# Zero fills beside two attentions on ScalarE's queue, first expert's weights loaded in the routing, first rows on ScalarE's queue, biases added after the rows

## The chip, the cores and the metric

The kernel runs on one core of one Trainium2 chip. The metric is the device time of one execution in microseconds (us); lower is better. Of the kernel before there are three timed executions and one profiled one. Engines are named as in the profile: PE is TensorE, PEld its weight load, DVE is VectorE, ACT is ScalarE, POOL is GpSimd, SP is SyncE; a q behind the name means its sequencer, which issues DMAs.

## The reference

Four layers, each a cross attention and a feed-forward part, are added one after the other to `x` (16 batches, 112 rows, 256 wide); the context `ctx` has 16 batches of 375 rows. All is float32. Cut to the parts that the change touches:

```python
# layer 0: focused linear attention (top 11 of 16 per head), then 8 experts, gated
x = x + L0_xattn(layernorm(x), ctx)
xn = layernorm(x) * ln_gamma + ln_beta
top_v, top_i = top_k(xn @ router_w.T, 2);  top_p = softmax(top_v)
slot = e * 560 + pos if pos < 560 else E * 560       # pos: place within expert e, C = 560
buf = zeros(E * C + 1, D).at[slot].set(xn[tokens])   # unused slots stay zero
g, u = split(buf[e] @ w12[e].T);  yb = (silu(g) * u) @ w3[e].T
x = x + scatter_add(yb[slot] * top_p * kept)
# layer 1: tanh-capped attention, shared feed-forward with low-rank terms
# layer 2: softmax attention, 16 heads of 64, K and V from ctx @ w_kv; then
logits = x' @ router_w.T + router_b                  # x' = layernorm(x), top 2 of 8, softmax
out = sum over chosen e of (gelu(x' @ w1[e].T + b1[e]) @ w2[e].T + b2[e]) * cw
x = x + layernorm(out + x') * ln_w + ln_b            # eps 1e-12
# layer 3: softmax attention, 16 heads of 16, with bq, bk, bv, bo; then a ternary feed-forward
x = x + softmax(q k.T / 4) v @ Wo.T + bo
```

## The kernel before

The program is a row of stages, each a block in which every engine runs its own instruction list; a stage ends when all engines have ended it. `x_sb` holds all 16 batches on chip with the 112 rows on the partitions. In order of time, from the span's start: focused attention of layer 0 (0 to 311 us), routing of layer 0 (311 to 426), experts of layer 0 (to some 870), tanh attention, shared experts, wide softmax attention of layer 2 (1255 to 1882), routing of layer 2 (1883 to 2003), experts of layer 2 (2004 to 2271), narrow attention of layer 3 (from 2277), ternary feed-forward (2683 to the end).

**Spilled keys and values.** The wide attention needs K and V of 1024 columns for each batch. For batches 0 to 7 PE projects them early, in holes of the focused attention (batches 0 to 3) and in the routing of layer 0 (batches 4 to 7); `SpilledKeysValues` does it. For each batch there are 8 parts of K and 6 of V: PE projects a part (L2375, L2379), ACT copies it out of the bank (`take`, L2396 and L2399) into a slot `ks` or `vs`, and SP stores the whole batch to DRAM (`serve`: one store `kd` of 1500 KB, L2342, and three stores `vd` of 500 KB, L2347). There are `SLOTS = 3` slots each; before ACT writes the first part of batch b it waits until the store of batch b - 3 has landed. The K store has 128 partitions, each V store 125.

**Routing** (`route`, for layers 0 and 2; `twice` is true for layer 0). SP loads the small weights, lets the K and V helper load its first contexts, then fills the expert input buffer `xbuf` in DRAM (4480 rows of 256) with zeros: four stores of 1120 KB from a tile `zeros` of 128x2240 that POOL has cleared (L2502). It waits until all four have landed, and only then serves the keys and values. The helper in layer 2's routing is `KeysValues`, which keeps K and V of layer 3 for some batches on chip and loads one context tile after the other (L2246), PE projecting at L2263 and L2268. DVE picks the two experts of each row and works out the slots, and POOL then writes the rows to `xbuf` by 32 indirect stores (L2516), after the zeros.

**Experts** (`run_experts`; `gated` is true for layer 0: 8 blocks of 560 rows; in layer 2 it is 35 blocks of 128 rows). SP, per block b: the rows of `xbuf` (L2755), then the up weights `wu` (L2758; 2048 KB in layer 0) and the down weights `wd` (L2760; 1024 KB), into two halves of each tile, h = b % 2. The first loads wait for nothing. PE transposes the rows (L2862), DVE copies them to `xT` (L2812), PE multiplies with `wu` (L2889), ACT and DVE form `hT`, PE multiplies with `wd` (L2874).

**Narrow attention** (`softmax_attention`, not wide) begins with the end of layer 2's experts: POOL gathers for each row its two experts' rows (`got`); DVE adds them with their weights to the input (L1305, L1307), takes mean and variance (L1310, L1311), ACT takes the root (L1185), DVE normalizes and adds to `x_sb` (L1322 to L1328), ACT takes the root of the next norm (L1190), and DVE makes `xn` (L1349, L1351), which PE transposes (L1480). Ahead of all of it DVE waits for all weights (`w_in`), clears a bank (L1296), waits for PE's eight bias matmuls (L1587) and adds the biases (L1298).

**Queues.** All DMAs named here are issued by SP, save the puts and gathers, which are POOL's. ACT issues none in these stages. An engine's instruction list is in program order; a scheduler does not reorder it.

## Time and profile before

| what | value |
|---|---|
| three timed executions | 2881.86, 2884.37, 2885.04 us; median 2884.37 |
| profiled execution, whole | 2856.36 us |
| its span | 2854.6 us |
| mean granted clock of PE, share of full speed | 0.944 |
| busy share of PE, DVE, ACT, POOL | 88%, 48%, 41%, 28% |

The profiled execution lies 28.0 us (1.0%) below the median of the timed ones. In the profile the times are microseconds from the span's start; a line "x <- y: total, times, longest" in the view of waits is idle time of x that ended when y came; the view of DMA issues gives when the issue starts and how long the sequencer was held by it, which is not the transfer.

### The profile page before, as it was taken

The page shows a single profiled execution, that of the slowest core. Times are in us where ns is not written, and L with a number is a line of the kernel's source. Part 1 is how long each engine was busy: PE and PEld are TensorE (multiplying, and loading weights), DVE is VectorE, ACT ScalarE, POOL GpSimd, SP SyncE. Part 2 cuts the span into 40 slices and gives each one's busy share as a digit, 9 for nine tenths or more (in the row PEclk, how much of TensorE's full clock was granted, in tenths as well). Part 3 has the DMA queues.
Part 4 walks back from the last instruction along what each step waited for, and adds up shares of the span by engine and source line. Part 5 has one row for each costly group of instructions (what it writes and reads, how often), then busy time and mean ns, then how long its engine had stood idle before and what let it go on. Part 6 is the DMA issues. An engine that isn't in the chain of part 4 may idle for free. (4 is left out here: it accounts for less than half of the span.)

```text
span 2854.6 us, 46446 instructions
## 1 busy us (share of the span) xinstructions
PE 2507.7 (88%) x15874; PEld 1765.5 (62%) x15874; DVE 1375.6 (48%) x4867; ACT 1158.1 (41%) x2651; POOL 801.9 (28%) x867
## 2 busy tenths in 40 slices
PE   5999786999986897979999999979899878889776
PEld 4766445888863454647765656556799746656544
DVE  6998511222215654546653333435011078887665
ACT  4556231111107992224444343423333346566331
POOL 3444140000005220017764444514000132222242
PEclk8999897999998998989999999989999969999898
DMA  4232365222105210044210000033888610000000
GB/s 139 76 114 99 122 185 167 90 90 91 53 17 151 69 56 1 1 114 142 109 55 12 7 12 6 1 132 111 298 326 327 241 33 18 18 15 9 1 7 20
DMA packets 71602, 252.17 MB, mean 88 GB/s; under 512 B 16299, under 2 KB 31944, under 8 KB 54912
## 3 DMA queue, kind: packets, MB, share of 16 engines
q1 hardware_dynamic: 61656, 225.71, 23.0%
q0 software_dynamic: 9744, 23.87, 2.8%
q8 instruction: 114, 1.87, 0.3%
q14 instruction: 88, 0.72, 0.1%
HBM read 197.44 MB, written 52.10 MB: 87 GB/s over the span
## 5 line engine op out<-in xcount | busy, mean ns | idle before, releaser
L2889 PE MATMUL L_ffne_up<-L_ffne_xT,L_ffne_wu 128*128 128x128 f32 (+1 forms) x2144 | 390.5, 337 | 7.0 <-DMA L_ffne_wu<-in_L_ffn_up 6.8
L2889 PEld LDWEIGHTS L_ffne_up<-L_ffne_xT,L_ffne_wu 128*128 128x128 f32 x2144 | 328.3, 193 | 54.3 <-DMA L_ffne_wu<-in_L_ffn_up 7.6
L1141 POOL TENSOR_SCALAR L_xattn_p<-L_xattn_p,L_xattn_rec 112x375 f32<-112x375 f32 x256 | 311.8, 1225 | 0.0
L1529 PEld LDWEIGHTS L_xattn_pt<-ident,L_xattn_p 112*125 112x125 f32 x1536 | 202.5, 194 | 164.2 <-issue 78.9
L1529 PE MATMUL L_xattn_pt<-ident,L_xattn_p 112*125 112x112 f32 x1536 | 254.0, 295 | 39.9 <-DVE L_xattn_pt L1378 36.2
L2874 PE MATMUL L_ffne_dn<-L_ffne_wd,L_ffne_hT 128*112 128x256 f32 (+1 forms) x1200 | 266.3, 379 | 1.5 <-issue 1.5
L1361 DVE TENSOR_REDUCE L_xattn_least<-L_xattn_s 112x1 f32<-112x375 f32 x256 | 128.3, 543 | 284.7 <-PE L_xattn_s L1517 284.5
L1378 DVE COPY L_xattn_pt<-L_xattn_pt 125x336 f32<-125x336 f32 x448 | 210.3, 498 | 68.9 <-PE L_xattn_pt L1529 65.7
L2874 PEld LDWEIGHTS L_ffne_dn<-L_ffne_wd,L_ffne_hT 128*112 128x112 f32 (+1 forms) x1200 | 216.8, 183 | 39.7 <-issue 2.1
L2777 POOL DMA_DIRECT2D L_ffn_ybuf<-L_ffne_y x75 | 40.1, 535 | 673.1 <-DVE L_ffne_y L2827 412.2
L1249 ACT ACTIVATE L_xattn_p<-L_xattn_s,L_xattn_least 112x375 f32<-112x375 f32 x256 | 145.1, 570 | 186.2 <-DVE L_xattn_least L1361 186.1
L1249 ACT ACTIVATE L_xattn_p<-L_xattn_p,L_xattn_least 112x375 f32<-112x375 f32 x256 | 153.7, 601 | 126.3 <-DVE L_xattn_least L1367 126.0
L2799 ACT ACTIVATE L_ffne_sg<-L_ffne_up 128x280 f32<-128x280 f32 x128 | 51.6, 403 | 348.5 <-PE L_ffne_up L2889 348.5
L2801 ACT ACTIVATE L_ffne_hT<-L_ffne_up,L_ffne_b 128x128 f32<-128x128 f32 x280 | 98.8, 366 | 154.1 <-DMA L_ffne_b<-in_L_ffn_b 79.4
L1139 POOL TENSOR_TENSOR pool_tick<-ident 1x1 f32<-1x1 f32 x128 | 23.4, 183 | 480.7 <-DVE L_xattn_rec L1373 480.7
L1552 PE MATMUL L_xattn_o<-L_xattn_pt,L_xattn_v 125*64 125x112 f32 (+1 forms) x3072 | 152.9, 268 | 0.0
L2845 DVE TENSOR_TENSOR L_ffne_hT<-L_ffne_sg,L_ffne_up 128x280 f32<-128x280 f32 x128 | 57.1, 446 | 190.1 <-ACT L_ffne_sg L2799 190.1
L1367 DVE CUSTOM_DVE_ANT_0 L_xattn_p<-L_xattn_s,L_xattn_hide 112x375 f32<-112x375 f32 x256 | 131.0, 545 | 16.8 <-issue 12.1
L1552 PEld LDWEIGHTS L_xattn_o<-L_xattn_pt,L_xattn_v 125*64 125x64 f32 (+1 forms) x3072 | 109.5, 118 | 45.8 <-issue 26.2
L1517 PE MATMUL L_xattn_s<-L_xattn_kt,L_xattn_qt 64*112 64x375 f32 x512 | 116.4, 531 | 17.7 <-ACT L_xattn_p L1249 17.7
L1517 PE MATMUL L_xattn_s<-L_xattn_kt,L_xattn_qbd 64*112 64x375 f32 x512 | 110.3, 547 | 4.4 <-POOL L_xattn_qbd L1159 2.7
L695 ACT ACTIVATE ta_pT<-ta_pT,ta_hide_b,ta_cap 125x896 f32<-125x896 f32 x96 | 113.8, 1189 | 0.0
(364 smaller groups left out, 4509.0 us busy)
## 6 DMA issues: line engine op xcount, KB each, us to landing
L_ffne_wd<-in_L_ffn_down SPq DMA_DIRECT2D x43, 1024.0 KB, 4.8
L_ffne_wu<-in_L_ffn_up SPq DMA_DIRECT2D x35, 1024.0 KB, 5.3
L_ffne_wu<-in_L_ffn_up SPq DMA_DIRECT2D x8, 2048.0 KB, 7.5
L_xattn_kd<-L_xattnkvks SPq DMA_DIRECT2D x8, 1500.0 KB, 7.1
L_xattn_vd<-L_xattnkvvs SPq DMA_DIRECT2D x24, 500.0 KB
L_xattn_kt<-L_xattn_kd SPq DMA_DIRECT2D x8, 1500.0 KB, 6.8
L_xattn_v<-L_xattn_vd SPq DMA_DIRECT2D x8, 1500.0 KB
L_ffn_xbuf<-L_ffnr_zeros SPq DMA_DIRECT2D x8, 1120.0 KB, 13.1
```

What stands on the lines that cost most here:

```text
L695: act.activation(p, p, ACT.Exp, bias=hide_b[:, h, c % KT:c % KT + 1], scale=cap[0:KP, :]).then_inc(exp_done, 1)
L1141: p = pool.tensor_scalar(at_p(b, head), at_p(b, head), rec[:, h, head:head + 1], None, ALU.mult)
L1249: act.activation(at_p(b, head), src, ACT.Exp, bias=least[:, h, head:head + 1], scale=-1.0, accum_out=sums[:, h, head:head + 1]).then_inc(e ...
L1361: dve.tensor_reduce(low, s, AX.X, ALU.min).then_inc(low_done, 1)
L1367: dve.tensor_tensor_reduce(out=at_p(b, head), in0=s, in1=hide[:, h, :], scale=1.0, scalar=3e38, op0=ALU.add, op1=ALU.min, accum_out=low).t ...
L1378: dve.tensor_copy(pt_sb[:, head % RP, :, :], pt_ps[head % 2][0:KP, 0, 0:KT * S].rearrange("p (k s) -> p k s", k=KT)).then_inc(pt_done, 1)
L1517: m = pe.matmul(score_ps(b, n)[0:S, 0, 0:SK], q, k, start=True, stop=True)
L1529: m = pe.transpose(pt_ps[head % 2][0:KP, 0, kt * S:(kt + 1) * S], at_p(b, head)[:, kt * KP:(kt + 1) * KP], ident[0:S, 0:S])
L1552: m = pe.matmul(o_ps[n * VC:n * VC + dh, chunk // 4, chunk % 4 * S:(chunk % 4 + 1) * S], v, pt_sb[:, (head + n) % RP, kt, :], start=(kt == ...
L2801: act.activation(hT[:, h, f, q * RH:(q + 1) * RH], src, ACT.Gelu, bias=b1[:, h, f:f + 1]).then_inc(h_done, 1)
L2874: m = pe.matmul(dn_ps[i][0:TR, 0, 0:D], hT[:, h, f, t * TR:(t + 1) * TR], wd[:, h, f, :], start=(f == 0), stop=(f == FC - 1))
L2889: m = pe.matmul(up_ps[s % RING][k][:, 0, 0:RH], wu[:, h, c, k * FF + f * 128:k * FF + (f + 1) * 128], xT[:, h, c, q * RH:(q + 1) * RH], st ...
```

## The change

It has four parts.

1. **Zero fills.** `xbuf` of both layers and one tile of zeros (128x320, set once by POOL in the focused attention) become members of `Core`. A fill is still 1120 KB but now reads the small tile seven times. The four fills of layer 0 are issued by ACT in the focused attention, in turns 5, 7, 9 and 11, right behind the copy of qT; those of layer 2 by ACT in the wide attention, at the start of turns 8 to 11. SP in both routings neither fills nor waits for fills; POOL waits for the fills ahead of its puts.
2. **First weights of layer 0.** In the routing of layer 0 SP loads `wu` and `wd` of expert 0 where the fills stood. Their tiles now live from the routing on; `SLOTS` goes from 3 to 2.
3. **First rows.** In both layers' experts ACT issues the loads of rows of blocks 0 and 1, at the stage's start; SP issues rows from block 2 on, and in layer 0 no weights of block 0.
4. **Narrow attention.** DVE no longer waits for `w_in` and the bias matmuls ahead of the rows; it adds the biases behind the first two batches' sums, ahead of `xn`. ACT takes a root of one column first.

```diff
+    def fill(self, eng, pre, q):
+        flat = self.xbuf[pre].rearrange("(p n) d -> p (n d)", p=128)
+        eng.dma_start(flat[:, q * 2240:(q + 1) * 2240].rearrange("p (m w) -> p m w", w=320),
+                      self.zeros[:, :].unsqueeze(1).broadcast_to([128, 7, 320])).then_inc(self.filled[pre], 16)
...
+        FILL_AT = (5, 7, 9, 11)
...
+                    if b == FILL_AT[0]:
+                        act.wait_ge(zeros_done, 1)
+                    if b in FILL_AT:
+                        core.fill(act, "L0_ffn", FILL_AT.index(b))
                     take_part(b, 0)
...
+                else:
+                    act.wait_ge(tiny_done, 1)
+                    act.activation(std3[:, 0:1], tiny[:, :], ACT.Sqrt).then_inc(warm, 1)
+                    act.wait_ge(warm, 1)
                 act.wait_ge(q_in, 48)
...
-                    act.wait_ge(tiny_done, 1)
                     root_of_sums(0)
                     root(0)
...
                 def body(b, h):
+                    if wide and 8 <= b < 12:
+                        core.fill(act, "L2_ffn", b - 8)
...
                     dve.memset(tiny[:, :], 1e-12).then_inc(tiny_done, 1)
-                    dve.wait_ge(w_in, NLOADS * 16)
                     dve.memset(o_ps[:, 0, :], 0.0).then_inc(pad_done, 1)
-                    dve.wait_ge(bias_out, 1)
-                    dve.tensor_tensor(bias_y[:, :], free_ps[FREE - 1][0:S, 0, 0:D], bias_y[:, :], ALU.add).then_inc(bias_done, 1)
-                    dve.wait_ge(bias_done, 1)
...
                     for b in range(2):
                         add_normed(b)
+                    dve.wait_ge(w_in, NLOADS * 16)
+                    dve.wait_ge(bias_out, 1)
+                    dve.tensor_tensor(bias_y[:, :], free_ps[FREE - 1][0:S, 0, 0:D], bias_y[:, :], ALU.add).then_inc(bias_done, 1)
+                    dve.wait_ge(bias_done, 1)
                 normalize(0, 0)
...
-    SLOTS = 3
+    SLOTS = 2
...
-                sp.wait_ge(setup, 2)
-                flat = r.xbuf.rearrange("(p n) d -> p (n d)", p=128)
-                for q in range(4):
-                    sp.dma_start(flat[:, q * fill_w:(q + 1) * fill_w], zeros[:, :]).then_inc(filled, 16)
-                sp.wait_ge(filled, 64)
+                if twice:
+                    sp.dma_start(r.wu[:, 0, :, :], ins[pre + "_up"][0]).then_inc(core.early_up, 16)
+                    sp.dma_start(r.wd[:, 0, :, :], ins[pre + "_down"][0]).then_inc(core.early_dn, 16)
                 keys.serve(sp, ins)
...
-                pool.wait_ge(filled, 64)
+                pool.wait_ge(core.filled[pre], 64)
...
-                    after(sp, t_out, (b - 1) * NT)
-                    sp.dma_start(rows[:, h, :, :], r.xbuf[bass.ts(b, R), :].rearrange("(t p) d -> p t d", p=TR)
-                                 ).then_inc(rows_in[h], 16)
-                    after(sp, up_out, (b - 1) * UPB)
-                    sp.dma_start(wu[:, h, :, :], ins[pre + "_up"][e]).then_inc(up_in[h], 16)
-                    after(sp, dn_out, (b - 1) * NT)
-                    sp.dma_start(wd[:, h, :, :], ins[pre + "_down"][e]).then_inc(dn_in[h], 16)
+                    if not isinstance(b, int) or b >= 2:
+                        after(sp, t_out, (b - 1) * NT)
+                        load_rows(sp, b, h)
+                    if not gated or not first(b):
+                        after(sp, up_out, (b - 1) * UPB)
+                        sp.dma_start(wu[:, h, :, :], ins[pre + "_up"][e]).then_inc(up_in[h], 16)
+                        after(sp, dn_out, (b - 1) * NT)
+                        sp.dma_start(wd[:, h, :, :], ins[pre + "_down"][e]).then_inc(dn_in[h], 16)
...
             def _(act):
+                load_rows(act, 0, 0)
+                load_rows(act, 1, 1)
```

SP's list at the end of layer 0's routing and the start of its experts, before (the branches are the stage's end and the next one's start):

```order
75 L2342 DMA L_xattn_kd<-L_xattnkvks 128x3000
76 L2347 DMA L_xattn_vd<-L_xattnkvvs 125x1024 x3
77 L2482 UNCONDITIONAL_BRANCH
78 L2750 UNCONDITIONAL_BRANCH
79 L2755 DMA L_ffne_rows<-L_ffn_xbuf 112x5x256
80 L2758 DMA L_ffne_wu<-in_L_ffn_up 128x4096
81 L2760 DMA L_ffne_wd<-in_L_ffn_down 128x2048
82 L2755 DMA L_ffne_rows<-L_ffn_xbuf 112x5x256
83 L2758 DMA L_ffne_wu<-in_L_ffn_up 128x4096
84 L2760 DMA L_ffne_wd<-in_L_ffn_down 128x2048
```

The same place on SP after the change, down to the same weights:

```order
76 L2366 DMA L_xattn_kd<-L_xattnkvks 128x3000
77 L2371 DMA L_xattn_vd<-L_xattnkvvs 125x1024 x3
78 L2505 UNCONDITIONAL_BRANCH
79 L2778 UNCONDITIONAL_BRANCH
80 L2787 DMA L_ffn_wu<-in_L_ffn_up 128x4096
81 L2789 DMA L_ffn_wd<-in_L_ffn_down 128x2048
```

And ACT's list there after the change, where before the table load followed the branch at once:

```order
249 L2423 ACTIVATE L_xattnkvvs<-L_xattnkvr_ps 125x512 x6
250 L2505 UNCONDITIONAL_BRANCH
251 L2816 UNCONDITIONAL_BRANCH
252 L2774 DMA L_ffne_rows<-L_ffn_xbuf 112x5x256 x2
253 L2831 ACT_TABLE_LOAD
254 L2831 ACTIVATE L_ffne_sg<-L_ffne_up 128x280 x32
```

Both row loads left SP for ACT, and expert 0's two weight loads left this place.

ACT's list at the start of the narrow attention, before:

```order
1031 L1180 UNCONDITIONAL_BRANCH
1032 L1199 ACTIVATE L_xattn_bqs<-L_xattn_bq 128x2
1033 L1185 ACT_TABLE_LOAD
1034 L1185 ACTIVATE L_xattn_std<-mv,L_xattn_tiny 112x2
1035 L1190 ACTIVATE std<-mv,eps 112x2
1036 L1235 ACTIVATE L_xattn_xt<-L_xattn_s 128x112 x2
```

And after:

```order
1041 L1199 UNCONDITIONAL_BRANCH
1042 L1215 ACT_TABLE_LOAD
1043 L1215 ACTIVATE L_xattn_std<-L_xattn_tiny 112x1
1044 L1222 ACTIVATE L_xattn_bqs<-L_xattn_bq 128x2
1045 L1204 ACTIVATE L_xattn_std<-mv,L_xattn_tiny 112x2
1046 L1209 ACTIVATE std<-mv,eps 112x2
```

The table load moved from between `bqs` and the first root to the stage's start.

## Rows read from the trace of the kernel before

**Rows 1.** The page: busy time, share of the span and instructions by engine.
```profile
PE 2507.7 (88%) x15874; PEld 1765.5 (62%) x15874; DVE 1375.6 (48%) x4867; ACT 1158.1 (41%) x2651; POOL 801.9 (28%) x867
```

**Rows 2.** Waits of PE, 415 to 460 us, layer 0's experts opening.
```profile
PE L_ffne_t L2862 <- DMA L_ffne_rows<-L_ffn_xbuf: 31.7, 1, 31.7
PE L_ffne_up L2889 <- DMA L_ffne_wu<-in_L_ffn_up: 2.3, 1, 2.3
```

**Rows 3.** Timeline of SP's issues there: start us, us held, line, DMA.
```profile
418.91 6.28 SPq L2347 DMA_DIRECT2D L_xattn_vd<-L_xattnkvvs  x1
426.95 4.33 SPq L2755 DMA_DIRECT2D L_ffne_rows<-L_ffn_xbuf  x1
```

**Rows 4.** Windows (stretch, length, five engines' busy, PEclk, DMA share, GB/s); page's DMA landings.
```profile
428.00:432.00 4.00, 0.00 (x0) 0.00 (x0) 0.00 (x0) 0.24 (x1) 0.00 (x0) 0.50 0.33 115
...
L_ffne_rows<-L_ffn_xbuf SPq DMA_DIRECT2D x8, 560.0 KB, 6.7
```

**Rows 5.** Timeline of PE, then DVE, same place: first transposes, up matmuls, last copy.
```profile
450.00 2.88 PE L2862 MATMUL L_ffne_t<-ident,L_ffne_rows 112*128 112x112 f32 x10 [31.75 <-DMA L_ffne_rows<-L_ffn_xbuf]
455.20 7.08 PE L2889 MATMUL L_ffne_up<-L_ffne_xT,L_ffne_wu 128*128 128x280 f32 x17 [2.33 <-DMA L_ffne_wu<-in_L_ffn_up]
...
452.91 0.39 DVE L2812 COPY L_ffne_xT<-L_ffne_t 128x224 f32<-128x224 f32 x1 [0.35 <-PE L_ffne_t L2862]
```

**Rows 6.** Windows, same columns, layer 2's routing.
```profile
1904.00:1908.00 4.00, 4.00 (x29) 3.57 (x27) 1.56 (x6) 1.88 (x6) 0.00 (x0) 1.00 0.99 419
...
1912.00:1916.00 4.00, 3.28 (x9) 2.05 (x9) 0.00 (x0) 0.40 (x1) 0.00 (x0) 0.50 0.23 91
1916.00:1920.00 4.00, 4.00 (x17) 2.87 (x18) 1.33 (x6) 1.24 (x4) 0.00 (x0) 0.70 0.00 0
```

**Rows 7.** Timeline of SP in layer 2's routing; then waits of PE, 1900 to 1925 us.
```profile
1890.20 2.00 SPq L2502 DMA_DIRECT2D L_ffn_xbuf<-L_ffnr_zeros  x4
1909.60 13.42 SPq L2246 DMA_DIRECT2D L_xattnkvr_ctxT<-in_ctxT  x3
...
PE L_xattnkvr_ps L2263 <- issue: 4.5, 1, 4.5
```

**Rows 8.** Waits of PE, 2003 to 2022 us, layer 2's experts opening.
```profile
PE L_ffne_t L2862 <- DMA L_ffne_rows<-L_ffn_xbuf: 5.8, 2, 4.3
```

**Rows 9.** Timelines of DVE, ACT, POOL, narrow attention opening; landings of its first ten gathers.
```profile
2285.36 0.48 DVE L1296 MEMSET L_xattn_o<- 128x512 f32 x1 [8.17 <-DMA L_xattn_bias_y<-in_L_xattn_bo]
2289.09 0.42 DVE L1298 TENSOR_TENSOR L_xattn_bias_y<-L_xattn_s,L_xattn_bias_y 112x256 f32<-112x256 f32 x1 [3.24 <-PE L_xattn_s L1587]
2289.55 0.48 DVE L1305 SCALAR_TENSOR_TENSOR L_xattn_got<-L_xattn_got,L_ffn_p,L_ffn_xf 112x256 f32<-112x256 f32 x1
...
2298.84 0.17 DVE L1349 RECIPROCAL rstd<-std 112x2 f32<-112x2 f32 x1 [0.42 <-ACT std L1190]
...
2293.12 1.28 ACT L1185 ACT_TABLE_LOAD   x1 [12.69 <-DVEq L1313]
...
2279.13 0.95 POOL L1149 DMA_INDIRECT L_xattn_got<-L_ffn_ybuf,L_ffn_get  x1 [0.30 <-issue]
...
DMA to landing us min/median/max: 2.6/3.4/6.4
```

**Rows 10.** Line L2502, all eight fills: durations min/median/max in ns.
```profile
L2502 SPq DMA_DIRECT2D L_ffn_xbuf<-L_ffnr_zeros x8: 431/440/948, 316.3 to 1891.6; - x8
```

**Rows 11.** Timeline of ACT: focused attention turn 5; wide attention turn 8.
```profile
126.52 0.48 ACT L2396 ACTIVATE L_xattnkvks<-L_xattnkva_ps 128x375 f32<-128x375 f32 x1 [2.86 <-PE L_xattnkva_ps L2375]
...
1507.65 0.57 ACT L1249 ACTIVATE L_xattn_p<-L_xattn_s,L_xattn_least 112x375 f32<-112x375 f32 x1 [0.55 <-DVE L_xattn_least L1361]
```

**Rows 12.** Timeline of SP's V stores in layer 0's routing; then ACT's first V copy of batch 7.
```profile
377.87 1.45 SPq L2347 DMA_DIRECT2D L_xattn_vd<-L_xattnkvvs  x3
...
391.63 8.00 SPq L2347 DMA_DIRECT2D L_xattn_vd<-L_xattnkvvs  x3
...
409.76 0.60 ACT L2399 ACTIVATE L_xattnkvvs<-L_xattnkvr_ps 125x512 f32<-125x512 f32 x1 [1.29 <-PE L_xattnkvr_ps L2379]
```

More of the change, by code:

```diff
@@ L75, in __init__ @@
         self.shared_in = ctx.enter_context(nc.semaphore("shared_in"))
+        self.filled = {pre: ctx.enter_context(nc.semaphore(f"{pre}_filled")) for pre in ("L0_ffn", "L2_ffn")}
+        self.early_up, self.early_dn = (ctx.enter_context(nc.semaphore(f"early_{n}")) for n in ("up", "dn"))
         self.used = []
@@ L93, in __init__ @@
         self.one = self.sb(ctx, "one", [128, 1])
+        self.zeros = self.sb(ctx, "zeros", [128, 320])
+        self.xbuf = {pre: nc.dram_tensor(pre + "_xbuf", (4480, D), F32).ap() for pre in ("L0_ffn", "L2_ffn")}
     def sb(self, ctx, name, shape, dt=F32):
@@ L194, in hosted @@
                 yield spilled.first + at // PARTS, at % PARTS
+        zeros_done = sem("zeros")
+        FILL_AT = (5, 7, 9, 11)
         with nc.Block() as block:
@@ L245, in _ @@
                 pool.memset(ones[:, :], 1.0).then_inc(setup, 1)
+                pool.memset(core.zeros[:, :], 0.0).then_inc(zeros_done, 1)
                 def normalize(b):
@@ L956, in softmax_attention @@
             got_in = core.got_in["L2_ffn"][0:RING]
+            warm = sem("warm")
             ln_in, tiny_done, summed, var_done, root_done, stats_done = (
@@ L2412, in __init__ @@
         self.owner = core.sb(ctx, pre + "_owner", [1, blocks], I32)
-        self.xbuf = core.nc.dram_tensor(pre + "_xbuf", (rows * blocks, D), F32).ap()
+        assert rows * blocks == 4480
+        self.xbuf = core.xbuf[pre]
         self.ybuf = core.nc.dram_tensor(pre + "_ybuf", (rows * blocks, D), F32).ap()
@@ L2447, in route @@
         ones = sb("ones", [S, S])
-        fill_w = r.R * r.blocks * D // 128 // 4
-        zeros = sb("zeros", [128, fill_w])
         xn4 = sb("xn4", [S, 4, D])
@@ L2469, in route @@
         cum_ps = core.banks(ctx, pre + "r_cum", 2)
-        w_in, std_done, setup, chain, filled = (sem(n) for n in ("w_in", "std", "setup", "chain", "filled"))
+        w_in, std_done, setup, chain = (sem(n) for n in ("w_in", "std", "setup", "chain"))
         xn_done, x_out, x_done, l_out, l_done = (sem(n) for n in ("xn", "x_out", "x", "l_out", "l"))
@@ L2508, in _ @@
                 pool.memset(ones[:, :], 1.0).then_inc(setup, 1)
-                pool.memset(zeros[:, :], 0.0).then_inc(setup, 1)
                 if tw:
@@ L2669, in _ @@
                 pe.wait_ge(w_in, NW * 16)
-                pe.wait_ge(setup, 2)
+                pe.wait_ge(setup, 1)
                 def logits(b, h):
@@ L2720, in sem @@
             return core.sem(ctx, pre + "e_" + name)
-        wu, wd = sb("wu", [128, 2, DC, UP]), sb("wd", [128, 2, FC, D])
-        if not gated:
+        if gated:
+            wu, wd = r.wu, r.wd
+        else:
+            wu, wd = sb("wu", [128, 2, DC, UP]), sb("wd", [128, 2, FC, D])
             b1, b2 = sb("b1", [128, 2, FC]), sb("b2", [TR, E, D])
@@ L2736, in run_experts @@
             sem(n) for n in ("t_out", "t", "up_out", "sg", "h", "dn_out", "y"))
+        if gated:
+            up_in[0], dn_in[0] = core.early_up, core.early_dn
         stored = core.stored[pre]
@@ L2747, in last, with load_rows @@
             return isinstance(b, int) and b == N - 1
+        def load_rows(eng, b, h):
+            eng.dma_start(rows[:, h, :, :], r.xbuf[bass.ts(b, R), :].rearrange("(t p) d -> p t d", p=TR)
+                          ).then_inc(rows_in[h], 16)
         with nc.Block() as block:
@@ L2913, in routed_experts @@
                     keys.keep(core, kept)
+                    r.wu = core.sb(kept, pre + "_wu", [128, 2, DC, 2 * FF])
+                    r.wd = core.sb(kept, pre + "_wd", [128, 2, FC, D])
                     keys.hold(core, held)
```

## The prediction

> **What bounds the kernel now.** I read the busy shares first: PE works 88% of the span and no other engine over half of it [rows 1], so apart from the focused attention, where DVE sets the pace, time is lost where PE stands still. Next I read PE's waits at each place where a stage opens, and last who was behind each. Four places matter.
>
> At the opening of layer 0's experts PE waits 31.7 us for the first rows, and 2.3 us more for `wu` [rows 2]. SP is the first reason: its last V store of batch 7 holds it 6.28 us from 418.91, the stage changes, and the rows are issued at 426.95 and hold it 4.33 us more [rows 3]. They land when PE's transposes begin, at 450.00 [rows 5], 23 us after the issue, where the eight loads of that size have a median of 6.7 [rows 4]. 
>
> In layer 2's routing SP issues the fills at 1890.20 and the next context only at 1909.60, after they have landed; PE, full until 1908, has nothing for 4.5 us [rows 6, 7] and then runs below full clock. At the opening of layer 2's experts the first two loads of rows cost 5.8 us [rows 8]. In the narrow attention DVE is ready at 2285.36 but starts on the rows at 2289.55, behind the bias matmuls [rows 9].
>
> **The change part by part.** The terms are made against the profiled execution, 2856.36 us with a span of 2854.6.
>
> *Opening of layer 0's experts.* The rows now stand first in a queue of ACT's own. ACT is free at 426.95 as SP is, since both pass the same stage change. Of the 560 rows 5/16, 175, go through the five engines with the V stores. If each engine takes turns between the two queues, one 1 KB row against one 4 KB piece of the V store (1024 floats), 175 such pieces, 700 KB, pass with them: 6.1 us at 115 GB/s [rows 4]. Added to the median landing of 6.7 us that is 12.8, so the rows land at 439.8. From the first transpose to the end of the last copy it was 3.3 us (450.00 to 452.91 + 0.39), and then `wu` was late by 1.9 us (to 455.20) [rows 5]. `wu` and `wd` of expert 0 are now long there. The up matmuls start at 443.1 instead of 455.20: **12.1 us** gained. The bounds: the rows land at 450.0 as before, leaving 1.9; or after the 6.7 alone, at 433.7, making 18.2. I take the middle one, as two queues with one engine's time between them is all that I can derive, and it lies at neither end. Behind it on ACT's queue come block 1's rows, needed when expert 0's up matmuls are done, of which 17 take 7.08 us [rows 5] and an expert has over a hundred: hidden in all three cases. The two early weight loads, 3 MB, stand in the routing where 4.5 MB of fills stood, so the first contexts and stores find no more traffic than before.
>
> The Trainium skill (DMA: Bandwidth & Descriptors, Issuing engines are not separate DMA queues) says that starting DMAs on several engines only saves the sequencer's time, as they run on the same 16 engines; by that this term would be some 2 us and not 12, which is the first rival below. Another section of the page (Queues, rings and completion order) has each engine take turns between the queues it has work for, which is the forecast. No row of before tells them apart, as ACT issues nothing here.
>
> *Layer 2's routing.* The context load no longer waits for fills, so the idle 4.5 us go [rows 7]. What follows is also paid: in 1912 to 1916 PE is busy 3.28 us at 0.50 of its clock and in 1916 to 1920 4.00 us at 0.70 [rows 6], which loses 3.28 x 0.50 + 4.00 x 0.30 = 2.8 us. PE was at full clock and full load before the gap, and there is none now to lower it: **7.3 us**. Bounds: 4.5, if another load is late there and the clock falls all the same, and 7.3. DVE's and POOL's work behind it waits for PE's products and moves along.
>
> *Opening of layer 2's experts.* ACT's two loads go ahead of what SP issues, by less than one issue; of the 5.8 us [rows 8] I take **0.5 us**, bounds 0 and 2.
>
> *Narrow attention.* The gather of batch 0's second row starts at 2279.13, and the slowest of the first ten takes 6.4 us, so it is there at 2285.5; DVE is ready at 2285.36. It starts some 4.0 us earlier than 2289.55. ACT's table load of 1.28 us is made beforehand. The bias addition of 0.42 us goes behind the sums, where DVE waited 0.42 us for ACT's root anyway [rows 9]; by then, 5 us later, the bias matmuls are done. Sum **5.2 us**; bounds 4.3 (the gather is a bit later and the addition shows) and 5.4. PE's next work waits for `xn`, so all of this is on the path.
>
> *Costs.* Eight fill issues on ACT. The same transfers held SP 0.43 us, at most 0.95 [rows 10]. In the focused attention ACT then waits 2.86 us for PE (turn 5), which hides an issue whole; in the wide attention there are 0.55 us before the first exponential [rows 11], which hide 0.43. I take **0.5 us** in all, bounds 0 and 8 x 0.95 less what is hidden, 4 x (0.95 - 0.55) = 1.6, doubled to 3.3 for a transfer that meets others in the focused attention. The clearing of a small tile on POOL and one root on ACT stand where both wait. Two slots instead of three: ACT's first V copy of batch 7 is at 409.76 and now needs batch 5's V stores, issued by 379.3; before, it needed batch 4's. Alone, 1500 KB at 115 GB/s would end at 392.7. SP is held 8.00 us by batch 6's stores until 399.6, which says that the queue was full then [rows 12]. Nearest to that row, some microseconds before 409.76, I cost it at nothing; each microsecond beyond would hold ACT, and with it PE.
>
> Sum: 12.1 + 7.3 + 0.5 + 5.2 - 0.5 = 24.6 us, so 2831.8 us in the profiled execution. The profiled one lies 28.0 us under the median, 1%, which I leave as it is: 2884.4 - 24.6 is 2859.8, taken as **2860 us**, 0.85% faster.
>
> **The rivals.** *The rows land no earlier on ACT's queue.* For it: 23 us of landing where the five engines are the bound, and SP's issues held for microseconds, which could hold ACT's too. Against it: SP's queue alone explains the holding. Then 1.9 + 7.3 + 0.5 + 5.2 - 0.5 = 14.4, **2870 us**. *They land at once*, if the V stores leave room: 18.2 in place of 12.1, 30.7 in all, **2854 us**.
>
> *The issues on ACT are held as SP's are* (slower than before). SP's issues took 6.28 and 2.67 us each while V stores stood in the queue [rows 3, 12]. If ACT's fills were held 6.28 us each, the focused attention would pay 4 x (6.28 - 2.86) = 13.7, the wide one 4 x (6.28 - 0.55) = 22.9, and with the rows held as well the gain of 12.1 shrinks to 1.9. Costs of 36.6 against gains of 1.9 + 7.3 + 0.5 + 5.2 = 14.9 are 21.7 us more, **2906 us**. It decides from a mean issue of 3.6 us (8 x 3.6 = 28.8, less the hidden 4 x 2.86 + 4 x 0.55 = 13.6, is 15.2). Against it: the fills were held 0.95 at most, one behind another, and ACT's queue is empty when each is issued.
>
> *The change doesn't do what it says in layer 2's routing:* the context still comes late behind other loads, and the term falls to 0: 17.3 left, **2867 us**. Against it: those loads were issued ahead of the fills.
>
> **How the numbers follow.** The forecast gets 0.55, the first rival 0.18, rows at once 0.14, the missing gain in layer 2's routing 0.07, held issues 0.06. For low I add the upper bounds: 18.2 + 7.3 + 2 + 5.4 - 0 = 32.9, which is 2851.5, set at 2850 for the median's own spread of 3 us. For high the lower ones: 1.9 + 4.5 + 0 + 4.3 - 3.3 = 7.4, which is 2877; only with all of them at once, so 2876. The range of 2850 to 2876 leaves out the held issues and little else. About 0.2%, 5.8 us, is what a measurement of this kernel can tell from no change. Slower by more than that is held issues, 0.05, with 0.01 for their mild form; I give 0.06. Within it I put 0.06, a mixture of the first rival, a lost term and some holding; faster 0.88.
>
> **What would show it.** Right: PE's wait for the first rows shrinks from 31.7 to about 21 us and the wait for `wu` is gone; PE has no gap near 1908 and keeps the clock; in the narrow attention the first addition of rows follows the gather's landing, ahead of the bias addition, and no table load stands between the sums and the root. Wrong: the rows landing 20 us or more after their issue; ACT issues of over 1 us; a wait of ACT for a store at batch 7's first V copy; PE waiting for block 1's rows or for `wu` of expert 1, which would give the gain back later.

## The result

| | kernel before | changed kernel |
|---|---|---|
| 20 timed executions each, median | 2881.97 us | 2874.19 us |
| span of the profiled execution | 2854.6 us | 2873.6 us |
| mean granted clock | 0.944 | 0.945 |
| busy PE | 2507.7 us (88%) | 2517.1 us (88%) |

The ratio is 0.9969, with a 95% interval of 0.9958 to 0.9980: 9 us faster, where 24.6 were forecast. The two spans seem to say the opposite, 19 us slower. They can't be set beside each other: the changed kernel's profiled execution (2875.31 us) lies near its median, that of the kernel before 26 us under its own. Of the executions one of the kernel before (3807 us) and two of the changed one (2929 and 7532 us) took far longer, and the ratio leaves them out. Much of the missing 16 us and this riddle have the same source.

Stage by stage, in us (all traces of the two kernels; a chip's number where it is known; the first trace of each is from the first comparison). The second column starts at PE's last K/V matmul of layer 0's routing, the third runs from the wide attention's last matmul to the routing's last one, the fourth starts there, and the last ends where DVE starts `xn`:

| kernel, chip | puts' start to last K/V matmul | to first up matmul (layer 0) | layer 2's routing, PE | to first up matmul (layer 2) | first gather to `xn` (layer 3) |
|---|---|---|---|---|---|
| before, first | 43.5 | 36.9 | 122.8 | 8.6 | 21.2 |
| before, 8 | 43.5 | 40.3 | 123.0 | 7.9 | 21.0 |
| before, 11 | 43.5 | 37.5 | 122.9 | 8.2 | 20.8 |
| before, 2 | 69.9 | 19.3 | 133.7 | 8.1 | 20.5 |
| changed, 8 | 43.5 | 25.1 | 116.3 | 7.4 | 17.1 |
| changed, 11 | 43.5 | 29.7 | 117.0 | 7.8 | 16.7 |
| changed, first | 71.9 | 24.0 | 132.8 | 7.7 | 16.5 |
| changed, 10 | 69.6 | 23.7 | 136.2 | 7.7 | 15.9 |
| changed, 2 | 70.1 | 23.5 | 130.0 | 7.9 | 16.3 |
| changed, 4 | 70.2 | 23.7 | 131.2 | 7.4 | 17.2 |

The traces are of two kinds. In one the first column is 43.5 us to the tenth, in the other some 70, whichever kernel runs, and all traces of one chip with the puts in place are of one kind. I call the chips prompt and late below. Each chip was used in one comparison only, so whether the chip itself differs or something that held there at that time is not shown. The trace of the kernel before on which the prediction rests looks prompt; its timed executions, by their time, and the changed kernel's trace look late.

What happens on a late chip, in the changed kernel's trace. Waits of PE from 311 to 480 us (the changed file's lines lie some 20 to 30 further down; L2399 and L2403 are the projection of K and V, L2894 the first transposes):

```profile
PE L_ffne_t L2894 <- DMA L_ffne_rows<-L_ffn_xbuf: 20.5, 1, 20.5
PE L_xattnkvr_ps L2403 <- issue: 13.6, 3, 6.7
...
PE L_xattnkvr_ps L2403 <- ACT L_xattnkvvs L2423: 7.3, 1, 7.3
```

The first line answers to [rows 2]: 31.7 us have become 20.5, the number that was forecast, but by luck: on a late chip the kernel before waits 12.9 us there (b_fifth, below). The other two have no counterpart in the kernel before's first trace. Timeline of PE there, and then of ACT, each row with its start and length; PE projects one part of V per row, ACT copies it out:

```profile
395.08 1.98 PE L2403 MATMUL L_xattnkvr_ps<-L_xattnkvwv,L_xattnkvctxT 128*125 128x512 f32 x4 [2.26 <-issue]
404.41 3.78 PE L2403 MATMUL L_xattnkvr_ps<-L_xattnkvwv,L_xattnkvctxT 128*125 128x512 f32 x4 [7.35 <-ACT L_xattnkvvs L2423]
...
403.76 0.60 ACT L2423 ACTIVATE L_xattnkvvs<-L_xattnkvr_ps 125x512 f32<-125x512 f32 x1 [8.73 <-issue]
414.19 0.60 ACT L2423 ACTIVATE L_xattnkvvs<-L_xattnkvr_ps 125x512 f32<-125x512 f32 x1 [9.84 <-remote]
422.60 0.60 ACT L2423 ACTIVATE L_xattnkvvs<-L_xattnkvr_ps 125x512 f32<-125x512 f32 x1 [7.80 <-remote]
```

The part that PE ends at 397.06 is copied at 414.19, 17.1 us later, by an idle ACT that waits for nothing but PE's semaphore; the one that ends at 408.19 is copied at 422.60, 14.4 us later.
### The profile page after: what moved, and what is told of

Its sections match the earlier page's. It is cut to its first block and busy times, and to the rows that moved or that the text cites. A ratio compares the mean times of both kernels' runs of the same rounds, so it can differ in the third digit from the quotient of the medians.

```text
span 2873.6 us, 46447 instructions
## 1 busy us (share of the span) xinstructions
PE 2517.1 (88%) x15874; PEld 1766.6 (61%) x15874; DVE 1373.8 (48%) x4867; ACT 1158.6 (40%) x2652; POOL 798.6 (28%) x866
## 3 DMA queue, kind: packets, MB, share of 16 engines
q1 hardware_dynamic: 59064, 215.13, 21.8%
## 5 line engine op out<-in xcount | busy, mean ns | idle before, releaser
L2921 PE MATMUL L_ffne_up<-L_ffne_xT,L_ffn_wu 128*128 128x280 f32 x1024 | 252.0, 403 | 0.6 <-DVE L_ffne_xT L2844 0.6
L2921 PEld LDWEIGHTS L_ffne_up<-L_ffne_xT,L_ffn_wu 128*128 128x128 f32 x1024 | 193.6, 192 | 45.3 <-issue 0.9
L2921 PE MATMUL L_ffne_up<-L_ffne_xT,L_ffne_wu 128*128 128x128 f32 x1120 | 138.7, 278 | 5.2 <-DMA L_ffne_wu<-in_L_ffn_up 5.2
L2906 PE MATMUL L_ffne_dn<-L_ffn_wd,L_ffne_hT 128*112 128x256 f32 x640 | 139.5, 379 | 1.0 <-issue 1.0
L2921 PEld LDWEIGHTS L_ffne_up<-L_ffne_xT,L_ffne_wu 128*128 128x128 f32 x1120 | 135.3, 194 | 7.3 <-DMA L_ffne_wu<-in_L_ffn_up 5.6
L2906 PEld LDWEIGHTS L_ffne_dn<-L_ffn_wd,L_ffne_hT 128*112 128x112 f32 x640 | 113.2, 177 | 26.4 <-issue 1.4
```

Of the source, the lines that this page charges most:

```text
L2906: m = pe.matmul(dn_ps[i][0:TR, 0, 0:D], hT[:, h, f, t * TR:(t + 1) * TR], wd[:, h, f, :], start=(f == 0), stop=(f == FC - 1))
L2921: m = pe.matmul(up_ps[s % RING][k][:, 0, 0:RH], wu[:, h, c, k * FF + f * 128:k * FF + (f + 1) * 128], xT[:, h, c, q * RH:(q + 1) * RH], st ...
```

## The experiments

All ratios are to the kernel before on the same chip in the same comparison.

### Both kernels again, and the two halves of the change

The kernels b_again and a_again are the two kernels unchanged. In only_l0 the layer 2 fills, layer 2's first rows and the narrow attention are as before:

```diff
-                    if wide and 8 <= b < 12:
-                        core.fill(act, "L2_ffn", b - 8)
...
+                else:
+                    for q in range(4):
+                        core.fill(sp, pre, q)
+                    sp.wait_ge(core.filled[pre], 64)
```

and undo_l0 is its complement: fills, weights, rows and three slots of layer 0 as before,

```diff
-    SLOTS = 2
+    SLOTS = 3
...
-                if not isinstance(b, int) or b >= 2:
+                if gated or not isinstance(b, int) or b >= 2:
```

> The kernel before, unchanged, once more. The changed kernel's trace shows semaphore updates that arrive 6 to 17 us after the matmul or copy that made them, only while POOL's indirect DMAs run (391 to 424, 1991 to 2011 us); the trace of the kernel before (span 2854.6, some 26 us under its median) shows none. Theory A (the late updates strike both kernels, and the profiled execution of before was one that escaped): the time is near 2880, and this trace shows 15 to 50 us of such stalls in layer 0's or layer 2's routing. Theory B (they belong to the change): no stalls here, span near 2855.

> The changed kernel, unchanged, once more. Theory A: ratio 0.997, and the stalls stand in this trace too, perhaps at other places among the indirect DMAs (puts of layer 0 and 2, gathers of layer 1 and 3). Theory B: stalls at the same two places with the same size, 29 and 17 us.

> The kernel before with the layer 0 parts alone: fills in the focused attention, first weights in the routing, two slots, first rows on ACT's queue. If its term of 12 us is real and not given back: ratio 0.9958. If two slots or the fills on ACT give it back in a routing whose stores run late: 0.999 to 1.003.

> The changed kernel with the layer 0 parts taken back (fills, weights, rows and three slots as before), leaving the fills of layer 2 in the wide attention, layer 2's rows on ACT and the narrow attention's order. If those terms are real: 7.3 + 0.5 + 5.2 = 13 us, ratio 0.9955. If the stalls in layer 2's routing belong to the change: about 1.000.

Chip 8, a prompt one. The kernel before took 2858.7 us, its copy 0.9994 (0.9981 to 1.0006) of it. The changed kernel: 0.9937 (0.9919 to 0.9955), 18 us faster; traces 2853.5 and 2834.7 us, 18.8 apart. The layer 0 half alone: 0.9971 (0.9956 to 0.9987); the other half: 0.9962 (0.9947 to 0.9978). No late update in a routing in any of the four. So theory A as worded, that the kernel before's first trace was a lucky execution, was wrong in its detail: here 10 of 10 executions lie between 2851 and 2863 us. Nor is B right, as the changed kernel has no stalls here. It goes with the chip and not with the kernel.

On such a chip the forecast's steps stand, layer 0's with a doubt. In the traces the halves move their own columns alone: only_l0 has 25.7, 122.8, 7.9 and 21.8 us, undo_l0 32.6, 116.3, 7.6 and 16.5. But in undo_l0, whose layer 0 is arranged as before, the first rows land 18.7 us after their issue and not 22 to 26, so that the opening is 4 to 8 us shorter than in the three traces of the kernel before, and by the times the layer 0 half is worth 8 us (4 to 13), where 12 were forecast. Waits of PE in a_again, 415 to 460 us, and then the start of layer 2's routing to 1990 us:

```profile
PE L_ffne_t L2894 <- DMA L_ffne_rows<-L_ffn_xbuf: 21.6, 1, 21.6
PE L_ffne_up L2921 <- DVE L_ffne_xT L2844: 0.6, 1, 0.6
...
PE L_ffnr_xt L2703 <- DVE L_ffnr_xn L2588: 10.7, 1, 10.7
PE L_ffnr_lg L1889 <- DVE tw_wsum L1897: 5.0, 1, 5.0
PE L_xattnkvr_ps L2287 <- DMA L_xattnkvr_ctxT<-in_ctxT: 1.2, 1, 1.2
```

The wait for `wu` of [rows 2] is gone, and so is the gap of 4.5 us of [rows 7].

### A second pair, and the puts taken away

In b_noputs and a_noputs POOL issues 2 of the 32 indirect stores of each routing:

```diff
-                for b in range(NB):
+                for b in range(1):
...
-                pool.wait_ge(put_done, 16 * 2 * NB)
+                pool.wait_ge(put_done, 16 * 2)
```

> The kernel before, unchanged, as the partner of the next three. If the semaphore updates are late on this chip as in the changed kernel's first trace: time near 2880 and PE and ACT waits of 20 us or more in the routings; if not: 2858 and none.

> The changed kernel, unchanged. Where updates come on time: ratio 0.9935, as in the second comparison. Where they come late: 0.997, with the loss in the routings' puts.

> The kernel before with 2 of the 32 indirect stores in each routing; 30 are left out, so the experts work on rows that are mostly zero. Theory A (the updates are late because of the puts' DMAs): ratio 1.000 where the updates are on time, some 0.990 where they are late. Theory B (another cause): 1.000 in both.

> The changed kernel with the same 30 indirect stores left out in each routing. Theory A: 0.9935 on either kind of chip, so on a late one the gain against b_noputs is again some 18 us; theory B: as a_third.

Chip 11, prompt again. Copy of before: 0.9989 (0.9971 to 1.0008). The changed kernel: 0.9918 (0.9887 to 0.9949), 23 us; traces 21.9 us apart. Without the puts the kernel before needs 0.9944 (0.9924 to 0.9964), 16 us less (18 by the medians), though 1.000 was expected: in its trace the first rows land 17.6 us after their issue and not 22 to 26. The DMA records show a smaller backlog: 0.9 MB of the K and V stores' pieces still move while the rows land, where it is 1.7 to 1.8 MB in the kernel before.

The changed kernel gains only 6 us by it (0.9896), so against b_noputs it is 12 us faster and not the 18 that were expected. That was the first sign of the second cause, and it is on a prompt chip. First transposes and up matmuls of PE in b_noputs and in a_noputs:

```profile
439.33 2.88 PE L2862 MATMUL L_ffne_t<-ident,L_ffne_rows 112*128 112x112 f32 x10 [20.30 <-DMA L_ffne_rows<-L_ffn_xbuf]
445.21 4.11 PE L2889 MATMUL L_ffne_up<-L_ffne_xT,L_ffne_wu 128*128 128x280 f32 x10 [3.00 <-DMA L_ffne_wu<-in_L_ffn_up]
...
445.56 2.88 PE L2894 MATMUL L_ffne_t<-ident,L_ffne_rows 112*128 112x112 f32 x10 [21.99 <-DMA L_ffne_rows<-L_ffn_xbuf]
449.01 3.60 PE L2921 MATMUL L_ffne_up<-L_ffne_xT,L_ffn_wu 128*128 128x280 f32 x7 [0.57 <-DVE L_ffne_xT L2844]
```

PE waits longer for the first rows with the change than without it: on ACT's queue they land 19.8 us after their issue, on SP's 17.6. From the last K/V matmul to the first up matmul it is 25.4 us against 26.2, so the opening gains 0.8 us and not 12. The other three columns gain 4.5, 1.3 and 5.5, with it 12.1 in all, which agrees with the times.

### A late chip, and the first rows back on SP

In rows_sp layer 0's first rows are issued by SP again, ahead of expert 1's weights; the early weights and the fills stay.

```diff
-                    if not isinstance(b, int) or b >= 2:
+                    if gated or not isinstance(b, int) or b >= 2:
...
-                load_rows(act, 0, 0)
-                load_rows(act, 1, 1)
+                if not gated:
+                    load_rows(act, 0, 0)
+                    load_rows(act, 1, 1)
```

> The changed kernel with layer 0's first two row loads back on SP, behind the last V store and ahead of expert 1's weights; everything else of the change stays. Theory (each of the 16 engines takes turns between the two queues): the rows land some 20 us after their issue instead of 14 to 16, and the time is 5 to 8 us over the changed kernel's, ratio 0.995. Rival (the issuing engine makes no difference): same as the changed kernel, 0.9925.

> The changed kernel once more, as the partner of the run before it: 0.9925 where semaphore updates come on time; 0.997 and late updates in the trace where the kernel before needs 2880 us.

Chip 10, late: the kernel before needs 2885.4 us. The changed kernel: 0.9974 (0.9956 to 0.9993), as in the first comparison, with the same late updates at the same places. But with the rows on SP: 0.9944 (0.9924 to 0.9963), 10 us better than with ACT's queue. Both expectations for it were wrong; this is the experiment that made the second cause plain.

### Three arrangements of the first rows on one late chip

In wait_rows the rows stay on ACT's queue, and SP issues expert 1's weights when expert 0's rows have landed:

```diff
+                    if gated and isinstance(b, int) and b == 1:
+                        sp.wait_ge(rows_in[0], 16)
                     if not gated or not first(b):
```

> The kernel before, unchanged, as partner. On a chip whose semaphore updates come late under the puts: time near 2884, and its trace shows the same late updates in both routings, 25 to 30 us before layer 0's first transposes; so they are the chip's and not the change's. On the other kind: 2858.

> The changed kernel, unchanged. 0.9925 on a chip with updates in time, 0.997 on one with late updates.

> The changed kernel with layer 0's first two row loads on SP, ahead of expert 1's weights. On a late chip 0.9944 as before, since there the V stores are gone by then and on ACT's queue the rows only take turns with expert 1's 3 MB of weights; on the other kind the rows wait behind batch 7's V stores: some 5 us over the changed kernel, 0.994.

> The changed kernel, rows on ACT's queue, but SP issues expert 1's weights only when expert 0's rows have landed. If it is the turns with those weights that make ACT's rows late: the rows land some 9 us after their issue instead of 14 to 19, the time is 4 us under the changed kernel's on a chip with updates in time and 10 us under it on a late one. If the V stores alone set the landing: no difference.

Chip 2, late: the kernel before needs 2884.4 us, its copy 0.9989 (0.9980 to 0.9999). The changed kernel 0.9966 (0.9953 to 0.9978), rows on SP 0.9929 (0.9913 to 0.9946), waiting weights 0.9946 (0.9930 to 0.9963). The last is 6 us under the changed kernel, where 10 were expected.

The kernel before has the same stalls here. Timeline of ACT in b_fifth, lines of the kernel before:

```profile
399.64 0.60 ACT L2399 ACTIVATE L_xattnkvvs<-L_xattnkvr_ps 125x512 f32<-125x512 f32 x1 [5.19 <-remote]
405.20 0.60 ACT L2399 ACTIVATE L_xattnkvvs<-L_xattnkvr_ps 125x512 f32<-125x512 f32 x1 [4.96 <-remote]
415.00 0.60 ACT L2399 ACTIVATE L_xattnkvvs<-L_xattnkvr_ps 125x512 f32<-125x512 f32 x1 [9.20 <-issue]
```

and its waits of PE, 311 to 480 us, which answer to [rows 2]:

```profile
PE L_xattnkvr_ps L2379 <- issue: 14.3, 4, 6.0
PE L_ffne_t L2862 <- DMA L_ffne_rows<-L_ffn_xbuf: 12.9, 1, 12.9
...
PE L_ffne_up L2889 <- DMA L_ffne_wu<-in_L_ffn_up: 3.5, 1, 3.5
```

PE waits 12.9 us for the first rows, not 31.7. Timeline of SP in b_fifth, and under it of SP and of ACT in a_fifth, where the rows begin:

```profile
442.15 7.12 SPq L2347 DMA_DIRECT2D L_xattn_vd<-L_xattnkvvs  x3
450.26 0.37 SPq L2755 DMA_DIRECT2D L_ffne_rows<-L_ffn_xbuf  x1
...
453.42 0.36 SPq L2787 DMA_DIRECT2D L_ffn_wu<-in_L_ffn_up  x1
453.83 1.12 SPq L2789 DMA_DIRECT2D L_ffn_wd<-in_L_ffn_down  x1
...
453.43 1.67 ACTq L2774 DMA_DIRECT2D L_ffne_rows<-L_ffn_xbuf  x2
```

SP's V stores are no longer held: three in 7.12 us, paced by PE's parts, and the rows' issue takes 0.37 us where it took 4.33 [rows 3]. The stall between 391 and 424 us has let the stores of batches 5 and 6 drain, so batch 7's meet a short queue, and the rows behind them land 11.0 us after their issue. There is nothing left for a second queue to pass. But it has something new to share with: SP issues expert 1's 3 MB in the same microsecond as ACT the rows, and the rows, by turns with them, land 18.1 us after their issue.

The first transposes and up matmuls of PE, in a_fifth, rows_sp2 and wait_rows, one pair each:

```profile
471.58 2.87 PE L2894 MATMUL L_ffne_t<-ident,L_ffne_rows 112*128 112x112 f32 x10 [20.06 <-DMA L_ffne_rows<-L_ffn_xbuf]
475.02 3.60 PE L2921 MATMUL L_ffne_up<-L_ffne_xT,L_ffn_wu 128*128 128x280 f32 x7 [0.58 <-DVE L_ffne_xT L2844]
...
462.27 2.87 PE L2895 MATMUL L_ffne_t<-ident,L_ffne_rows 112*128 112x112 f32 x10 [12.74 <-DMA L_ffne_rows<-L_ffn_xbuf]
465.72 4.48 PE L2922 MATMUL L_ffne_up<-L_ffne_xT,L_ffn_wu 128*128 128x280 f32 x12 [0.58 <-DVE L_ffne_xT L2845]
...
457.89 2.88 PE L2896 MATMUL L_ffne_t<-ident,L_ffne_rows 112*128 112x112 f32 x10 [11.79 <-DMA L_ffne_rows<-L_ffn_xbuf]
461.34 4.07 PE L2923 MATMUL L_ffne_up<-L_ffne_xT,L_ffn_wu 128*128 128x280 f32 x8 [0.57 <-DVE L_ffne_xT L2846]
```

PE waits 20.1, 12.7 and 11.8 us. With the weights held back the rows land 9.8 us after their issue, on ACT's queue as well: what delays them there is what they share the engines with.

The traces' DMA records show it piece by piece, as K's pieces (12000 bytes), V's (4 KB), `wu`'s (16 KB) and `wd`'s (8 KB) differ in size. What else moved between the first rows' issue and their landing:

| trace | rows on | landing, us | K and V stores, MB | expert weights, MB |
|---|---|---|---|---|
| before, b_again, b_third | SP | 23.0, 25.7, 22.2 | 1.7, 1.7, 1.8 | 3.2, 3.2, 2.6 |
| undo_l0 | SP | 18.7 | 1.6 | 2.3 |
| b_noputs | SP | 17.6 | 0.9 | 3.5 |
| b_fifth, rows_sp2 | SP | 11.0, 10.8 | 0.7, 0.7 | 1.8, 1.0 |
| a_again, a_third | ACT | 14.1, 15.7 | 1.4, 1.3 | 2.1, 2.2 |
| a_noputs | ACT | 19.8 | 0.9 | 2.9 |
| a_fifth | ACT | 18.1 | 0.7 | 3.0 |
| wait_rows | ACT | 9.8 | 0.7 | 0 |

On SP's queue the landing grows with the backlog ahead of the rows. On ACT's it grows with the weights that pass beside them. In a_again and a_third SP's backlog still holds some of these weights back, and the rows land sooner than in a_noputs and a_fifth, where it doesn't.

### The same once more, and the puts taken away on a late chip

> The changed kernel, unchanged, as partner: 0.9925 on a chip with semaphore updates in time, 0.997 on one with late updates.

> Layer 0's first two row loads on SP, the rest of the change kept. On a chip with updates in time the V stores of batch 7 are still in SP's queue, so the rows land some 20 us after their issue instead of 14 to 16: 4 to 6 us over the changed kernel. On a late chip: 10 us under it.

> Rows on ACT's queue, expert 1's weights issued only when expert 0's rows have landed. On a chip with updates in time the rows then take turns with the V stores alone: they land 11 to 13 us after their issue, 2 to 4 us under the changed kernel. On a late chip: 6 us under it, as before.

> The kernel before with 2 of the 32 indirect stores in each routing, 30 left out, so the experts work on rows that are mostly zero. On a chip with updates in time 0.9944 as before. On a late one, if the late updates come from the puts' DMAs: both routings lose their stalls and the time falls to some 0.985; if not, to 0.994 again.

Chip 4, late: before 2884.3 us; changed 0.9948 (0.9928 to 0.9969), rows on SP 0.9940 (0.9915 to 0.9966), waiting weights 0.9939 (0.9920 to 0.9958). By the medians rows on SP and waiting weights are 5 and 3 us under the changed kernel, where 10 and 6 were expected, and the intervals overlap; in the traces the up matmuls start 23.7, 16.1 and 15.1 us behind the last K/V matmul, the same to 0.2 us as on chip 2.

Without the puts the kernel before needs 0.9860 (0.9841 to 0.9879) here, 41 us less by the medians, 2843.0 us, against 2843.6 on the prompt chip. Its timeline of PE over the stretch where the stalls were:

```profile
387.41 10.46 PE L2379 MATMUL L_xattnkvr_ps<-L_xattnkvwv,L_xattnkvctxT 128*125 128x512 f32 x24
397.71 10.27 PE L2375 MATMUL L_xattnkvr_ps<-L_xattnkvctxT,L_xattnkvwk 128*128 128x375 f32 x32
407.81 10.46 PE L2379 MATMUL L_xattnkvr_ps<-L_xattnkvwv,L_xattnkvctxT 128*125 128x512 f32 x24
```

PE runs through, and from the puts' start to the last K/V matmul it is 43.5 us again. The puts bring the late updates, and their absence makes the two kinds of chip equal. Whether it is their transfers or POOL's work on them is not separated here. Why ACT sees PE's parts late beside indirect stores on one chip and not on another is open, and none of these runs can tell.

## Why the prediction was wrong

2874.19 us lies at the upper end of the range, but a third of the forecast gain is not the forecast. By its steps:

**Opening of layer 0's experts, forecast 12.1: the step that failed.** On the prompt chips it roughly held: from the last K/V matmul to the first up matmul 38.3 us in the mean of three traces of before, 26.8 in the mean of a_again, a_third and only_l0 (25.7), so 11.5 gained; 10.0 if undo_l0's 32.6 is counted with the kernel before. In a_again the rows are issued at 428.21 and land 14.1 us later, where 12.8 were worked out. The sum left out expert 1's weights, of which 2.1 MB pass in that time; what the rows would need without them was not run on a prompt chip. On the late chips, where the comparison was made, the same stretch is 19.3 us in the kernel before and 23.5 to 24.0 in the changed one: **4.4 us lost instead of 12.1 gained**. That these 16.5 us are about what is missing in all (15.6) is in part luck, since layer 2's routing falls short too, and some gain is not placed. Two sentences of the prediction carry it. "The rows land at 450.0 as before" was the worst bound, and took the 23 us as a property of the kernel; they belong to a routing in which nothing stalls. And "Behind it on ACT's queue come block 1's rows" looked at what stands behind the rows on their own queue, but not at what SP, freed of them, would issue in the same microsecond. The prediction named that place among what would show it wrong, as a wait for expert 1's weights; it was the rows that waited for them.

The rule weighed there, of the Trainium skill (DMA: Bandwidth & Descriptors, Issuing engines are not separate DMA queues), that starting DMAs on several engines saves only the sequencer's time, comes out neither way. On the prompt chips the rows landed 14.0 to 15.7 us after their issue on ACT's queue and 18.7 to 25.7 on SP's, against it; on the late ones there was no gain. That all share the same 16 engines, as that section says, agrees with the late traces: 18.1 us beside 3 MB of weights, 9.8 without them.

**Layer 2's routing, forecast 7.3.** Prompt: 122.9 to 116.3 and 117.0, so 6.3. Late: 133.7 in the one trace of before, 130.0 to 136.2 in four of the changed kernel and in the five of rows_sp and wait_rows, which share this part, with a mean of 132.5. The late updates there vary by more than the term; what is left of it is between a loss of 3 and a gain of 4, in the mean 1.

**Layer 2's experts, forecast 0.5.** 8.2 to 7.6: 0.6.

**Narrow attention, forecast 5.2.** 20.9 to 16.6, so 4.3, on every chip. In a_again, rows of DVE, ACT and POOL that answer to [rows 9]:

```profile
2271.71 0.48 DVE L1325 SCALAR_TENSOR_TENSOR L_xattn_got<-L_xattn_got,L_ffn_p,L_ffn_xf 112x256 f32<-112x256 f32 x1 [8.64 <-DMA L_xattn_got<-L_ffn_ybuf,L_ffn_get]
2279.50 0.43 DVE L1457 TENSOR_TENSOR L_xattn_bias_y<-L_xattn_s,L_xattn_bias_y 112x256 f32<-112x256 f32 x1 [0.22 <-DVE mv L1348]
...
2262.34 1.28 ACT L1215 ACT_TABLE_LOAD   x1 [10.53 <-PEq L128]
...
2264.41 0.96 POOL L1168 DMA_INDIRECT L_xattn_got<-L_ffn_ybuf,L_ffn_get  x1 [0.30 <-issue]
```

DVE starts on the rows 7.3 us after the second gather's issue, not 6.4: the largest of ten landings was no bound for another trace. The bias addition shows for 0.2 us. The sum itself, 4.0 and 1.28, makes 5.3 and not 5.2.

**Costs, forecast 0.5.** None can be seen: the eight fills hold ACT 0.38 to 0.45 us each (line L114 of a_again):

```profile
L114 ACTq DMA_DIRECT2D L_ffn_xbuf<-zeros x8: 378/385/446, 123.4 to 1641.2; - x8
```

and the turns of the focused attention keep their length: between the starts of the first and the last of DVE's 16 products `fa_kv` it is 246.6 us in the first trace of before, 246.8 in a_again. The puts of layer 0 do start later, at 378.2 us in the mean of thirteen traces with the fills moved (375.6 to 381.4) against 376.1 in seven without (374.4 to 379.6); half of these 2 us are there at 30 us already (DVE's first instruction of the focused attention, 30.3 against 29.3), ahead of the first fill, so a cost of 1 us can be neither shown nor excluded. The wide attention takes 621.9 to 624.4 us in the kernel before, 621.9 to 624.3 in the changed one. Two slots cost nothing either, on both kinds of chip: ACT's first V copy of batch 7 waits as long for PE in the changed kernel's first trace as it did before [rows 12], and for no store:

```profile
441.53 0.60 ACT L2423 ACTIVATE L_xattnkvvs<-L_xattnkvr_ps 125x512 f32<-125x512 f32 x1 [1.29 <-PE L_xattnkvr_ps L2403]
```

In a_again the same copy waits 1.29 us for PE, too. The prediction misread one row on the way: that SP was held 8.00 us by batch 6's stores [rows 12]. The row spans three issues, held 0.25, 0.25 and 1.13 us; in between SP waited for ACT's next parts. So it says little on a full queue, and the 2.67 us each of the rival with held issues were no holding.

So 11.5 + 6.3 + 0.6 + 4.3 = 22.7 us on a prompt chip, measured 18 and 23. Stages that the change does not touch differ by some us from trace to trace: PE's stretch in the tanh attention is 216.3 and 216.7 us in a_again and a_third and 213.7 to 214.6 in three traces of before, but 217.0 in b_fifth and 214.6 in a_noputs. On a late chip -4.4 + 0.4 + 4.3 is 0.3, and with layer 2's routing some 1 to 2 us, 4 at most; measured are 8, 9, 10 and 15. The rest is not placed. Part of it may lie in which executions were profiled: the changed kernel's four late ones took 1 to 7 us more than their medians (a_fifth 2881.3 against 2874.0), b_fifth 2 us less than its own and 5 less than that of all executions of the kernel before there. A stall that varies from one execution to the next can't be shared out from single traces.

The step before all others was wrong too: "the profiled one lies 28.0 us under the median, 1%, which I leave as it is". By b_fifth that 1% was no scale factor. It was two stalls of 26 and 11 us (69.9 against 43.5, 133.7 against 122.9), less the 18 us by which the opening behind the first is shorter, and some us of other stages. They were in the executions that were to be predicted and not in the trace that was read, one of them right ahead of the largest term. It was the one number on the page that spoke against the sum.

## What to carry to other kernels

When a profile's own time differs from the median by more than the effects to be judged, ask where the difference sits before costing anything: a stall upstream lets queues drain, and a wait for a backlog is then not there to be saved. When a load moves to a second queue, list what both queues hold in the same microseconds: a small urgent load by turns with megabytes of weights is later than one that stands ahead of them in a single queue. The best arrangement here was the least clever: first rows at the head of SP's queue with the weights behind them, or the weights held until the rows have landed, 11 and 6 us under the changed kernel on chip 2, 0.9929 and 0.9946 of the kernel before, and 5 and 3 us on chip 4, where the intervals overlap. Which of the two is better is not shown, and on a prompt chip neither was run.

## What the runs showed of the hardware

On three chips of five by number (10, 2 and 4, against 8 and 11), each used once, and in the changed kernel's first trace, ACT sees some of PE's parts up to 17.6 us late while POOL's indirect stores run: 26 us of stall in layer 0's routing and some 11 in layer 2's. With the stores left out the stalls of the routings are gone and 41 us with them; on a prompt chip the same stores cost 16 to 18. A load of 560 KB landed 9.8 us after its issue on ACT's queue with nothing new on SP's, and 18.1 us after it beside 3 MB of weights there. Fills of 1120 KB on ACT's queue held the sequencer 0.4 us each, and no slowing beside them can be told from the spread of the traces.
